# A fused audio-tower kernel: two expert tiles in the first round and three in the last, and q and k projected ahead of the first turn of expert inputs

## The reference

```
h = concat over patch sizes 8, 16, 32 of (patches(x) @ W.T + b + pos + scale_emb)   # [16, 221, 128]
h = h + attention(layernorm(h))         # 8 heads of 16, softmax over the 221 tokens of a sequence
h = h + moe(layernorm(h))               # applied to the first 1024 tokens' routing
# moe: 2 of 8 experts for each token: gelu(x @ w1[e]) @ w2[e], 512 hidden, weighted and added
```

## Time and profile before

| | |
|---|---|
| median of 3 runs | 252.54 us (252.16 to 252.75) |
| profiled execution, its own time | 252.67 us |
| its span (first to last instruction) | 250.0 us |
| PE busy | 239.3 us, 96% of the span |
| DVE, ACT, POOL busy | 185.1, 138.9, 133.7 us |
| chain that ended last | PE 86%, DMA 4%, DVE 4% |
| granted clock of PE | 1.000 |

### The profile page before, as it was taken

The page is one execution under the profiler, slowest core; times in us unless marked ns, Lnnn a source line. Parts: engine busy times, 40 slices in busy tenths (PEclk is TensorE's granted clock), DMA queues, the critical chain, the costliest instruction groups (busy, mean ns, idle before and its releaser), DMA issues.

```text
span 250.0 us, 6983 instructions
## 1 busy us (share of the span) xinstructions
PE 239.3 (96%) x2703; PEld 198.8 (80%) x2703; DVE 185.1 (74%) x417; ACT 138.9 (56%) x223; POOL 133.7 (53%) x181
## 2 busy tenths in 40 slices
PE   7999899999999999999998999999999999999992
PEld 6899879777686788797777888888888888877671
DVE  3898646959796879788765786878787877866743
ACT  4771230744344343544464958787877778787450
POOL 7000066140747465767574375867777877673422
PEclk9999999999999999999999999999999999999999
DMA  6999603314638483942415318272636363535222
GB/s 208 409 393 399 273 21 92 86 25 91 206 84 241 96 244 88 240 118 59 119 33 131 90 22 163 33 162 34 134 60 151 47 141 42 122 41 116 37 21 47
DMA packets 30192, 32.00 MB, mean 128 GB/s; under 512 B 3831, under 2 KB 26695, under 8 KB 30129
## 3 DMA queue, kind: packets, MB, share of 16 engines
q1 hardware_dynamic: 25214, 28.17, 39.4%
q0 software_dynamic: 4080, 2.59, 8.2%
q10 hardware_dynamic: 866, 0.81, 1.0%
HBM read 16.24 MB, written 5.95 MB: 89 GB/s over the span
## 4 chain that ended last, share of the span: by engine, by line
PE 86%; DMA 4%; DVE 4%; issue 2%; ACT 1%; POOL 1%; DVEq 0%
PE s_ps L1288 16%; PE e_ps L1212 14%; PE s_ps L1212 11%; PE m_ps L1405 9%; PE e_ps L1485 8%; PE m_ps L1471 5%; PE m_ps L1273 5%; PE e_ps L1471 2%; PE m_ps L1279 2%; PE m_ps L1434 2%; DMA w_raw<-wt 2%; DMA z_slots<-z,slot_u 1%; PE m_ps L1262 1%; PE m_ps L1280 1%; PE m_ps L1435 1%
## 5 line engine op out<-in xcount | busy, mean ns | idle before, releaser
L994 DVE TENSOR_REDUCE nmax<-s_ps 104x4 fp32r<-104x884 f32 (+1 forms) x60 | 61.9, 1073 | 10.1 <-PE s_ps L1288 9.9
L684 ACT ACTIVATE probs<-s_ps 104x888 f32<-104x888 f32 (+1 forms) x60 | 51.2, 905 | 26.8 <-PE s_ps L1288 26.7
L571 POOL DMA_INDIRECT out<-y_sb,idx_u x23 | 36.4, 1582 | 33.5 <-DMA out<-y_sb,idx_u 26.3
L1288 PE MATMUL s_ps<-pair_a 32*104 32x222 f32 (+1 forms) x504 | 37.8, 307 | 0.5 <-ACT probs L684 0.5
L1288 PEld LDWEIGHTS s_ps<-pair_a 32*104 32x104 f32 (+1 forms) x504 | 24.5, 169 | 13.7 <-issue 8.8
L501 POOL TENSOR_TENSOR var_eps<-mv,eps_t 128x2 f32<-128x2 f32 x16 | 6.0, 378 | 49.0 <-DVE mv L959 48.9
L534 POOL DMA_INDIRECT z_slots<-z,slot_u x20 | 22.1, 1107 | 15.2 <-PE s_ps L1288 11.3
L1405 PE MATMUL m_ps<-probs,v_aug 104*32 104x221 f32 (+1 forms) x480 | 25.8, 353 | 0.0
L1485 PE MATMUL e_ps<-w_now,hidT 128*128 128x128 f32 x184 | 23.2, 276 | 0.0
L1485 PEld LDWEIGHTS e_ps<-w_now,hidT 128*128 128x128 f32 x184 | 21.7, 192 | 0.2
L745 ACT ACT_TABLE_LOAD x16 | 20.5, 1283 | 0.3
(11 more groups left out here) (165 smaller groups left out, 532.8 us busy)
## 6 DMA issues: line engine op xcount, KB each, us to landing
pair_a<-qk SPq DMA_DIRECT2D x64, 111.0 KB
w_sb<-w SPq DMA_DIRECT2D x8, 512.0 KB, 4.3
pair_b<-qk SPq DMA_DIRECT2D x30, 111.0 KB
w_raw<-wt SPq DMA_DIRECT2D x6, 512.0 KB, 10.5
x_raw<-x SPq DMA_DIRECT2D x6, 512.0 KB, 9.4
z_slots<-z SPq DMA_DIRECT2D x1, 1518.0 KB, 13.5
zs<-z_slots SPq DMA_DIRECT2D x7, 198.0 KB, 3.3
x_raw<-x SPq DMA_DIRECT2D x4, 256.0 KB, 4.7
```

Of the source, the lines that this page charges most:

```text
L571: g.indirect_dma_start(rows, bass.IndirectOffsetOnAxis(ap=idx_u[:, at:at + 1], axis=0), y_sb[:, n % 2, i, :], None, compute_op=ALU.add).th ...
L684: s.activation(probs[0:n, blk, 2 * f:2 * f + 2].rearrange("p t u n -> p t (u n)"), s_ps[0:n, 2 * f:2 * f + 2, 0:2 * NE], ACT.Exp, scale=DH ...
L994: v.tensor_reduce(nmax[0:n, blk, 2 * f:2 * f + 2, MAX_ROW[0]:MAX_ROW[1] + 1:2], src, AX_X, ALU.max, negate=True).then_inc(max_ready, 1)
L1288: mm = pe.matmul(dst[0:n, i, u * NE:(u + 1) * NE], a[rs, u, N0 * blk:N0 * blk + n], b[rs, u, :], start=start, stop=stop)
```

## The change

`ROUND_TILES` gives round 0 (cycle 7) two tiles and round 7 (cycle 14) three. In cycle 7, PE does `project_qk(8)` ahead of `zs_turn(0)`, and ACT does `qk_high(8)` ahead of `first_zsT_copy`. In cycle 14, ACT does all of `last_y` after both `exps`, and PE does `down(7, 2)` behind `project_v(15)`.

```diff
-ROUND_TILES = (3, 3, 3, 3, 3, 3, 3, 2)
+ROUND_TILES = (2, 3, 3, 3, 3, 3, 3, 3)
@@ ACT, in the loop over cycles
                 if n > 0:
                     gelu(n, 0)
-                if n == 0:
-                    first_zsT_copy()
                 if n >= 0:
                     qk_high(c + 1)
                 if n == 0:
+                    first_zsT_copy()
                     gelu(n, 0)
@@
                 if 0 <= c < BATCH:
                     exps(c, 0)
-                if n == ROUNDS - 1:
-                    last_y(0)
                 if 0 <= c < BATCH:
                     exps(c, 1)
                 if n == ROUNDS - 1:
-                    last_y(1)
+                    for i in range(ROUND_TILES[n]):
+                        last_y(i)
@@ PE, in the loop over cycles
-                if n == 0:
-                    zs_turn(0)
                 if ahead1:
                     project_qk(c + 1)
                 if n == 0:
+                    zs_turn(0)
                     hidden(n, 0)
@@
-                if n < ROUNDS - 1:
-                    down(n, 2, ROUND)
+                down(n, 2, ROUND)
```

## The result

The changed kernel takes 254.38 us (median of 10 runs, 253.31 to 257.19) where the kernel before takes 252.64 us beside it. The ratio is **1.0082**, 95% interval 1.0053 to 1.0112: slower by 0.8%, about 2 us, where 1.1 us was forecast. The ratio leaves out a few executions in a second, slower state, so it is not quite that of the medians. The profiled execution took 253.49 us with a span of 251.3, which is 1.3 us more than the span before.

A forecast was written before the change was run, and what follows sets the result against it. PE was taken to pace the expert cycles, with POOL's add queue at its limit behind it. Last add 246.2 + 3.6 + 1.3 = 251.1 span, +1.1 on 252.54: 253.6 us; 8-in-10 range 251.6 to 255.1.

The forecast's parts named there:

- An add into cycle 15: POOL's add queue: one add more in cycle 15, nothing hides it; last add leaves at 246.2, span +1.1 us.
- The end's tail: Program end: SP passes its wait 3.6 us after the last add's issue, the span ends 1.3 us later.
- The compute path: Up to the last store: 2.0 us gained early, 0.5 lost in cycle 14, net -1.5 us; last store leaves at 244.8.
- The tile out of cycle 7: PE, cycle 7: tile saves 1.9 us, new stall before `zs_turn(1)` costs 0.6; in all cycle 8 starts 2.0 earlier.
- q and k first: Cycle 7: `project_qk(8)` fills PE's 1.12 us idle wait; `hidden(0,0)` begins 0.2 us earlier, `qk_high` ahead of the copy costs 0.
- POOL in cycles 7 and 8: POOL waits longer at `fetch_w1(1,2)`, but w1 and w2 copies arrive 1.5 us early; cost 0, up to 1 us.
- The tile into cycle 14: Cycle 14: third `hidden` and `down(7,2)`, 0.89 us each, fill PE's waits; compute path's end 0.5 us late.
- the signs of being wrong: A last add before 244.6, an end set by the stores, or `hidden(0,0)` starting over 0.5 us earlier.
- The rival with the compute path at the end: Program end: last add leaves at 244.0 or earlier, total 251.0 to 251.5 us, faster by 1.1 to 1.5; chance 0.18.
- the tie: Program end: queue lag 1.7 us, last add at 245.4, end at 250.3; total 252.8 us, give or take 0.4; chance 0.12.
- The cover that goes costs more: Stall at `zs_turn(1)` and POOL's cycle 8 wait hit PE; the 2.0 us gain becomes 1.0, total 254.6 us; chance 0.10.

The follow-up runs named there:

- the second profile of the changed kernel: The changed kernel unaltered, timed and profiled again beside the kernel before, on one chip with variants of the change: ratio 1.0102 of the kernel before.
- the last experiment: The changed kernel with its adds to `out` made plain writes of the same rows: ratio 0.9950 of the kernel before.

## Why the prediction was right, and where it was not

**The direction and its cause held.** "An add into cycle 15. This is the term that decides": the last add was forecast at 246.2 and left at 245.96, SP passed its wait at 249.3 where 249.8 was forecast. Taking that one add away gives about 2.6 us back, adding one to the kernel before costs 4.7, and taking the tile from a round that doesn't shorten the queue's start costs nothing that the runs can tell.

**The issue of 246.2 held by two errors that cancel.** Round 6's first add was written at 225.0 and left at 224.81. But the gate was written as 222.7 and was 223.26, since PE was 1.5 us early and not 2.0 by then. The lag behind it was written as 2.3 and was 1.55. That add was not held by the scores at all (its wait is 0.17 us, for nothing that the profile shows, behind POOL's w2 copies), so a time worked out from the gate could be right only by luck. In the second profile of the changed kernel it left at 226.63. The steps behind it, 4.16, 4.11, 4.83, 4.01, 4.04, sum to 21.15, where 21.2 was written with other single steps (4.69, 4.30, three times 4.08). In the second profile they sum to 21.39, so this sum is the firm part.

**The end's tail was mis-sized.** "The end is 1.3 us behind SP's last wait": it was 2.0 behind, since POOL's drain ends 1.8 us after the landing. The 1.3 had been measured in the kernel before between SP's wait for the stores and an end that was already the drain's. From the last issue to the end 4.9 us was written; it was 5.6 in the kernel before (244.41 to 250.0) and 5.3 in the changed one. With the end of the kernel before read as the adds', the forecast for the same issue would have been 246.2 - 244.41, 1.8 us instead of 1.1. The two profiles differ by 1.3, the medians by 1.7, the ratios give 2.1 to 2.6. The profiled execution of the changed kernel was one of its fastest (253.49 us with a median of 254.38), and in the second profile the last add left at 248.02. How the rest divides between such scatter and the steps below is open.

The tail of the stores was mis-sized too, the other way: 3.7 us from the last store's issue to the end (246.31 to 250.0). In the runs that the stores ended it was 2.3 to 2.6 (246.37 to 248.7, 248.02 to 250.6). So the compute path had more in hand than the forecast gave it.

**The compute path gained less than forecast**: the last store leaves 0.8 us earlier in the first pair of profiles, where 1.5 was written, and 0.26 of it were there before cycle 7 began (its first scores start at 127.66 instead of 127.92). Even this is one pair. Over all profiles with the changed tiles and POOL's order as it was the last store leaves between 245.50 and 248.02, and in the ones of the kernel before with an add fewer or more at 246.66 and 246.67. By steps:

- *The tile out of cycle 7.* Cycle 8 starts 2.36 us earlier, 2.1 of it from the change; 2.0 was written. The firm part is what lies behind the start of `hidden(0,0)`: 1.67 us, where 1.6 was written (1.9 + 0.3 - 0.6), with the new stall in front of `zs_turn(1)` at 0.61 in each profile. The part ahead of it, 0.43 us here, is luck. It is not there in the other profiles, where cycle 8 starts at 142.03 to 142.52 with two tiles and the old place of the adds.
- *q and k first.* Written: "It costs 0 if that holds and 0.3 if the rows land early; I take 0." The rows landed early: the turn ended at 132.31 and ACT's copy began at 132.56, behind `qk_high`, where before it began 0.04 us behind the turn. That is the 0.3 or a little less; with the copy itself PE waited 0.67 us. Not written was that in the old order the projection covers the copy, so that the new order loses by rows that are early. An estimate: SP's loads went out at 128.43 and landed after 2.3 to 3.1 us, by 131.5 at the latest, and 1.1 us behind a turn PE could have begun `hidden(0,0)`, by 132.6 and not at 132.99. `hidden(0,0)` still started 0.69 us earlier than before (133.68). By its number this is one of the signs of being wrong ("over 0.5 us earlier"). But 0.26 us of it came before cycle 7, and the loads went out 1.5 us earlier than before (128.43 against 129.91), which was not forecast and is not so in the other profiles (130.1 to 130.8).
- *POOL in cycles 7 and 8.* "Cost 0" was wrong by 0.9 us in this profile (the lead of 2.36 us at the start of cycle 8 is 1.48 at the projections of cycle 9), and in another place than the one bounded. The w1 copy came at 144.91, the w2 copies by 147.9, both in time. But DVE's residual was late for `pv` (0.29 us), and then POOL's late copies stretched DVE's short instructions. The runs with the copy freed show that the wait of `fetch_w1(1,2)` is behind what is lost after the projections of cycle 8, 0.4 us here.
- *The tile into cycle 14.* 0.66 us was added from the projection there (223.26 against 224.73) to the last output products (244.40 against 245.21), where 0.5 was written. The stalls that it fills were filled: of the waits in the earlier trace rows only the 0.32 for the q maxima is left.

**The Trainium skill's rule** on the page "DMA: Bandwidth & Descriptors", section "Anatomy of one DMA — SWDGE (gpsimd) path" (an estimate of 2.15 us here), stands well with the plain write of the last experiment, 2.4 us. It does not hold for the accumulating transfer, 3.4 us. By it the compute path would have set the end, and with plain writes it did.

The rival with the compute path at the end named 244.6 as the issue from which it decides; with the two tails as measured it is nearer 243 (245.50 + 2.6 - 5.3). Of the others, the tie did not come about. *The cover that goes costs more* did in part: cycle 8 lost 0.9 us, and in the second profile round 1's first add was late by 1.9 us against the first, 1.1 of it from ahead of cycle 7, with an end at 253.4.

## What to carry to other kernels

- A serial queue of transfers has a clock of its own. Count its steps from the last place where it had time to spare to the end of the program; work moved across that place adds a whole step (4 us here, of which half was left in the total), even if every engine gains.
- Read the closing drain of the engine that issues indirect transfers beside the last waits: here it ends 5.1 to 5.4 us behind the last add's issue, 1.8 behind the landing, and is part of the time. Whether it waits for the landing is open: behind the plain write it ends 4.5 us behind the issue, and with adds and with plain writes alike 3.5 us behind the end of the issuing instruction (3.9 in the kernel before).
- When a queue on one engine is moved, look at what else of that engine slides, and beside which instructions of its neighbour it comes to lie.
- Before work is moved into a wait, look for the wait in a second profile. The 1.12 us in cycle 7 were there in one execution and not in two others with the same cycle 7.

## What the runs showed of the hardware that was not expected

Accumulating in the transfer costs 1.0 us of landing and 0.6 us of issue for 64 KB (medians of 23: 3.4 against 2.4 and 1.58 against 1.0).

Short DVE instructions beside GpSimd's copies of 128 by 512 numbers took 0.99 and 1.73 us instead of 0.16 and 0.22. The Trainium skill's page "SBUF — State Buffer", section "Who interferes with whom", counts DVE's `copy` and `tensor_scalar` among the operations that can contend with GpSimd for a shared port pair, under conditions on their operands, and has the pair held by one instruction to its end. The trace agrees in that just such two instructions were stretched beside GpSimd's copies; that the port pair is the reason, no run here shows.
